# First stage of a transformer block: q, k and v from two fp32r parts in three products, the norm on ScalarE

## The chip, the cores and the metric

One core of a Trainium2 chip runs the whole program. The metric is the device time of one execution, in microseconds.

## The reference

```python
h = _layernorm(x, axis=-1) * (1 + ca) + sa
x = x + ga * _L0_attn_ref(h, w_qkv, w_proj, b_proj)
...
def _L0_attn_ref(x, w_qkv, w_proj, b_proj):
    qkv = (x @ w_qkv).reshape(B, S, 3, heads, head_dim)
    Q, K, V = (qkv[:, :, 0], qkv[:, :, 1], qkv[:, :, 2])
    Q = apply_rope(Q)
    K = apply_rope(K)
    ...
```

`x` is (4, 2048, 256) in f32, `w_qkv` (256, 768), and there are 16 heads of 16. Attention, the projection and a mixture of experts follow; they are the other stages of the kernel and are left as they are, but for the increments named below. The change bears on the layer norm, its modulation with `ca` and `sa`, and the product with `w_qkv`.

## The kernel before

The program is a row of stages: setup (`setup_stage`), q, k and v (`qkv_stage`), attention, middle (projection, second norm, routing), experts, shared expert. Each stage is a block of its own, which begins on all five engines when the one before has ended. Within a stage every engine has its own list of instructions, in an order written out by hand, and semaphores tie them together.

`qkv_stage` goes over 16 units of 512 tokens (4 batches, 4 units each), and a unit over 4 tiles of 128 tokens. `steps_of` (L308) calls `run` once a unit on each engine; batches 1 and 2 are a hardware loop. Within `run`, step t handles several tiles at once: `tile(t, k)` is the tile k steps back, of this unit or the one before. What a tile goes through:

- `products` (TensorE, L614), step n: h times `wqkv`, 2 chunks of 128 for q and k (512 columns, to `ps_qk`) and 2 for v (256 columns, to `ps_v`), in f32. It waits for the rotation of the tile two before and for `h_t` of its unit.
- `rope` (VectorE, L513), step n: the rotation, three operations out of `ps_qk` into `rot_c` and `rot_s`.
- `take_v` (ScalarE, L563), step n: v out of PSUM. `add` (GpSimd, L464), step n: the sum of the two halves of the rotation, `qk`.
- `turn_qk` (TensorE, L628), two steps later: four transposes of `qk` into `ps_x`, which has two slots. It waits for `rest` of the tile two before it.
- `first` (ScalarE, L570), two steps later, `leave` (VectorE, writes `rest`, L528), `second` (ScalarE, L577) and `third` (GpSimd, L470), three steps later: q and k split into three bf16 parts.

Once a unit, for the next unit: `stat` (VectorE, L493) takes mean and variance, `rstds` (GpSimd, L457) the reciprocal root, `normalise` (VectorE, L504) writes `xn`, `turn_h` (TensorE, L605) transposes it with eight transposes into `ps_ht`, and `modulate` (ScalarE, L555) writes `h_t`, two activations of 128x512. Before the change `stat` stands after the rotation of tile 0, `rstds` after the sum of tile 0, `normalise` after step 1 of VectorE, and `turn_h` at the end of step 2 of TensorE:

```python
def run(b, s, more, tile):      # VectorE, L535
    for t in range(TPS):
        if tile(t, 0):
            rope(b * SPB + s, t, s * TPS + t)
        if t == 0 and more:
            stat(b * SPB + s + 1, (s + 1) % SPB, b + ((s + 1) // SPB + 1))
        if tile(t, 3):
            u, tt, slot, _ = tile(t, 3)
            leave(u, tt, slot)
        if t == 1 and more:
            normalise(b * SPB + s + 1, (s + 1) % 2, (s + 1) % SPB)
```

`stand_alone` (L161) is an increment of a semaphore that nobody waits for.

## Time and profile before

| | us |
|---|---|
| median of 3 runs (lowest to highest) | 3309.3 (3305.76 to 3310.84) |
| the profiled execution, its own time | 3308.82 |
| its span, from first to last instruction | 3307.1 |
| PE busy (TensorE matmul) in the span | 2912.5 (88%) |
| DVE busy (VectorE) | 2518.0 (76%) |
| ACT busy (ScalarE) | 1588.5 (48%) |
| POOL busy (GpSimd) | 884.5 (27%) |
| mean granted TensorE clock, share of full speed | 0.944 |

The shares of the whole span mix six stages. The first stage runs from 29.4 us to near 300; the first 40 us of it and the last 20 are its ends. A busy PE is not PE at its peak, since matmuls are pipelined and their ends are modelled. Spans on POOL are rough. In rows, idle time and what ended it stand in brackets behind an instruction.

### The profile page before, as it was taken

How to read it: one execution, taken by the hardware profiler on the slowest of the kernel's cores; microseconds unless marked ns; L12 is line 12 of the kernel's file. 1: busy time of each engine (PE TensorE's matmuls, PEld its weight loads, DVE VectorE, ACT ScalarE, POOL GpSimd, SP SyncE). 2: the span in 40 equal slices, each digit the busy share in tenths (PEclk: the TensorE clock that was granted, in tenths of full speed). 3: DMA queues.
4: the chain of work that ended last, by engine and by line, in shares of the span. 5: the costliest groups of instructions: out<-in, count | busy, mean ns of one | idle time of the engine just before them, and what ended most of it. 6: DMA issues, size and time to landing. Idle time of an engine off the chain costs nothing. (4 is left out here: it accounts for less than half of the span.)

```text
span 3307.1 us, 61435 instructions
## 1 busy us (share of the span) xinstructions
PE 2912.5 (88%) x22508; PEld 1616.0 (49%) x22508; DVE 2518.0 (76%) x4678; ACT 1588.5 (48%) x2160; POOL 884.5 (27%) x1100
## 2 busy tenths in 40 slices
PE   6885699999999999999999996873999999788888
PEld 3553133333333333333333325763888888677776
DVE  5885989888898888898888914664777777566665
ACT  2542166666676666666666782221444444111111
POOL 5773010111110111101111112664222222333332
PEclk8997699999999999999999997775999999899999
DMA  4776111122111212111221005664444455332332
GB/s 132 204 209 186 49 35 47 48 54 53 43 44 49 54 48 57 38 46 48 55 52 43 20 8 160 212 198 167 155 155 155 156 159 156 105 94 85 96 97 73
DMA packets 388533, 317.93 MB, mean 96 GB/s; under 512 B 112720, under 2 KB 374844, under 8 KB 388288
## 3 DMA queue, kind: packets, MB, share of 16 engines
q1 hardware_dynamic: 370752, 277.67, 29.4%
q0 software_dynamic: 12288, 33.57, 3.0%
q10 hardware_dynamic: 5248, 3.41, 0.4%
q8 instruction: 155, 2.54, 0.3%
q14 instruction: 90, 0.74, 0.1%
HBM read 196.89 MB, written 116.93 MB: 95 GB/s over the span
## 5 line engine op out<-in xcount | busy, mean ns | idle before, releaser
L903 ACT ACTIVATE probs<-ps_s 128x1024 f32<-128x1024 f32 (+3 forms) x1280 | 1077.9, 896 | 599.2 <-PE ps_s L1071 598.6
L926 DVE TENSOR_REDUCE piece_rest<-ps_m 128x1 f32<-128x512 f32 (+2 forms) x1260 | 748.8, 646 | 91.8 <-PE ps_m L1046 42.0
L1071 PE MATMUL ps_s<-q_st,k_st 50*128 50x512 bf16 (+7 forms) x5120 | 594.4, 346 | 19.0 <-ACT probs L903 15.2
L1086 PE MATMUL ps_o<-probs,vs 128*32 128x512 f32 (+3 forms) x5120 | 600.8, 541 | 4.3 <-POOL probs L883 1.2
L883 POOL TENSOR_SCALAR_AFFINE_SELECT probs<-probs 128x256 f32<-128x256 f32 x512 | 204.9, 406 | 1481.2 <-ACT probs L903 1476.0
L926 DVE TENSOR_REDUCE piece_late<-ps_m 128x1 f32<-128x512 f32 x900 | 548.8, 666 | 33.0 <-PE ps_m L1038 17.9
L1038 PE MATMUL ps_m<-k_st,q_st 48*128 48x512 bf16 (+3 forms) x2400 | 407.5, 353 | 65.8 <-DVE piece_rest L926 48.1
L1038 PEld LDWEIGHTS ps_m<-k_st,q_st 48*128 48x128 bf16 x2400 | 106.9, 93 | 651.8 <-DVE piece_rest L926 339.0
L1071 PEld LDWEIGHTS ps_s<-q_st,k_st 50*128 50x128 bf16 (+1 forms) x5120 | 224.1, 95 | 250.8 <-ACT probs L903 91.0
L1803 ACT ACTIVATE act_g<-ps_g 128x512 f32<-128x512 f32 x117 | 69.9, 597 | 279.5 <-PE ps_u L1895 279.5
L1840 DVE TENSOR_TENSOR hid_f<-act_g,ps_u 128x512 f32<-128x512 f32 x117 | 80.5, 688 | 126.8 <-ACT act_g L1803 126.8
L1086 PEld LDWEIGHTS ps_o<-probs,vs 128*32 128x32 f32 x5120 | 101.2, 108 | 142.8 <-issue 96.9
L2086 ACT ACTIVATE act_g<-ps_g 128x512 f32<-128x512 f32 x80 | 47.5, 595 | 251.1 <-PE ps_u L2191 206.3
L1765 POOL TENSOR_TENSOR wu_low<-wu,wu_high 128x768 fp32r<-128x768 f32 x39 | 76.8, 1968 | 326.1 <-ACT wu_high L1791 326.1
L2202 PE MATMUL ps_d<-sd_high,hid_high 128*128 128x256 f32 x384 | 114.0, 297 | 47.5 <-DVE hid_low L2135 46.2
L1359 POOL DMA_INDIRECT expert_rows<-rows,at x128 | 133.3, 1041 | 66.9 <-issue 36.0
L1845 DVE TENSOR_TENSOR hid_low<-hid_f,hid_high 128x512 fp32r<-128x512 f32 x117 | 138.8, 1187 | 4.0
L2051 POOL DMA_INDIRECT got<-expert_made,at_now x128 | 128.7, 1006 | 49.1 <-issue 36.8
L1907 PE MATMUL ps_d<-wd_high,hid_high 128*128 128x256 f32 x468 | 136.0, 291 | 1.2 <-DVE hid_low L1845 1.2
L1907 PE MATMUL ps_d<-wd_low,hid_high 128*128 128x256 f32 x468 | 132.1, 282 | 0.0
L1907 PE MATMUL ps_d<-wd_high,hid_low 128*128 128x256 f32 x468 | 132.0, 282 | 0.0
L621 PE MATMUL ps_qk<-wqkv,h_t 128*128 128x512 f32 x256 | 122.8, 603 | 1.0 <-ACT h_t L559 1.0
(228 smaller groups left out, 5103.2 us busy)
## 6 DMA issues: line engine op xcount, KB each, us to landing
k_st<-qk_parts SPq DMA_DIRECT2D x768, 32.0 KB, 1.8
qk_parts<-parts SPq DMA_DIRECT2D x124, 192.0 KB, 2.9
q_st<-qk_parts SPq DMA_DIRECT2D x720, 32.0 KB, 1.8
x_r<-expert_rows SPq DMA_DIRECT2D x39, 512.0 KB, 4.6
expert_made<-made SPq DMA_DIRECT2D x39, 512.0 KB, 2.9
x_in<-in_L_attn_x_dram SPq DMA_DIRECT2D x32, 512.0 KB, 4.7
vs<-v_ones SPq DMA_DIRECT2D x64, 256.0 KB, 3.7
v_ones<-v_out SPq DMA_DIRECT2D x60, 256.0 KB, 4.7
```

The costliest lines, as they stand in the source:

```text
L621: pe.matmul(ps_qk[:, t % 2, :], h_t[:, slot, c, t * P:(t + 1) * P], wqkv[:, c, 0:QK], start=(c == 0), stop=(c == DC - 1))
L883: pool.affine_select(out=block_now, in_=block_now, compare_op=ALU.is_ge, fill=0.0, base=0, pattern=[[0, 2], [1, P]], channel_multiplier=-1 ...
L903: act.activation(probs[:, u % PSLOTS, 2 * pair:2 * pair + 2, j * P:ST], ps_s[:, pair, :, j * P:ST], ACT.Exp, scale=SCALE).then_inc(exp_don ...
L926: v.tensor_reduce(dst, ps_m[:, bank, 0:n * w].rearrange("p (n w) -> p n w", n=n), AX.X, ALU.max) \
L1038: last[z] = pe.matmul(bank[:, i * w:(i + 1) * w], q_st[rows, slot, 0, a + i, qi * P:(qi + 1) * P], k_st[rows, slot, 0, a + i, kt * ST:kt * ...
L1071: last = pe.matmul(ps_s[:, pair, z, j * P:ST], k_st[rows, slot, half, pair, kc * P:(kc + 1) * P], q_st[rows, slot, half, pair, qt * ST + j ...
L1086: last = pe.matmul(ps_o[h * VW:(h + 1) * VW, j * P:ST], vs[:, slot, kc, h * VW:(h + 1) * VW], probs[:, u % PSLOTS, h, j * P:ST], start=(kc ...
L1359: pool.indirect_dma_start(rows_dram, bass.IndirectOffsetOnAxis(at[:, rslot, j:j + 1], 0), rows[:, rslot, j % TPS, :], None).then_inc(scatt ...
L1845: v.tensor_tensor(hid[1][:, i, :], hid_f[:, half, :], hid[0][:, i, :], ALU.subtract).then_inc(hid_done, 1)
L1907: last = pe.matmul(ps_d[:, t, :], hid[a][:, i, t * P:(t + 1) * P], wd_p[b][:, slot, i, :], start=(i == 0 and t % 2 == 0 and k == 0), stop= ...
L2051: pool.indirect_dma_start(got[:, slot, j, :], None, made_dram, bass.IndirectOffsetOnAxis(at_now[:, slot, j:j + 1], 0)) \
L2202: last = pe.matmul(ps_d[:, slot, t, :], hid[a][:, i % GS, t * P:(t + 1) * P], wd_p[b][:, i, :], start=(i == 0 and t % 2 == 0 and k == 0), ...
```

## The change

`wqkv` and h are each split into two fp32r parts, "high" (rounded) and "low" (the remainder), and the product is taken as high x high + high x low + low x high: six matmuls where two f32 matmuls stood, for q and k and for v. For it `modulate` writes h twice (`h_p[0]` in fp32r and `h_f` in f32), now one chunk at a time, the first at the end of step 1 and the second in step 2, and `low_rows` on VectorE subtracts the two at the end of step 2, one 128x512 operation a chunk; `products` waits for it. The weights are split in the setup stage, on ScalarE and GpSimd.

The norm goes from VectorE to ScalarE, as `x * rstd + shift`, at the start of step 0. VectorE only makes `shift`, four elements a partition, at the start of step 0 before `rope`; `xn` has one slot. `stat` and `rstds` work two units ahead, in step 3: `stat` before the rotation of tile 3, `rstds` after the sum of tile 3, where it also waits for the norm before. `turn_h` goes from the end of step 2 to the end of step 1. In the middle and the shared stage all increments of `held` are taken out (six places).

```diff
-                    wqkv=first.enter_context(nc.sbuf_tensor("wqkv", [P, DC, 3 * D], F32)),
+                    wqkv=[first.enter_context(nc.sbuf_tensor(f"wqkv_{part}", [P, DC, 3 * D], F32R)) for part in PARTS],
+                    w_raw=first.enter_context(nc.sbuf_tensor("wqkv_raw", [P, DC, 3 * D], F32)),
...
+            pool.wait_ge(masks, 6)
+            pool.wait_ge(exp_done, 2)
+            pool.tensor_tensor(Q["wqkv"][1][:, :, :], Q["w_raw"][:, :, :], Q["wqkv"][0][:, :, :], ALU.subtract)
...
+            act.wait_ge(Q["consts"], 16 * 3)
+            act.activation(Q["wqkv"][0][:, :, :], Q["w_raw"][:, :, :], ACT.Copy).then_inc(exp_done, 1)
...
-        xn = sb("xn", [P, 2, TPS, D])
-        h_t = sb("h_t", [P, 2, DC, ST])
+        xn = sb("xn", [P, TPS, D])
+        h_p = [sb(f"h_{part}", [P, 2, DC, ST], F32R) for part in PARTS]
+        h_f = sb("h_f", [P, DC, ST])
+        shift = sb("shift1", [P, TPS])
...
                 pool.wait_ge(pool_own, u + 3)
+                if not (isinstance(u, int) and u == 0):
+                    pool.wait_ge(xn_done, u * TPS)
+                    stand_alone(pool, held)
                 pool.tensor_tensor(rstd[:, :], var[:, :], power[:, :], ALU.pow).then_inc(rstd_done, 1)
...
-                    if t == 0 and more:
-                        rstds(b * SPB + s + 1)
+                    if t == 3 and has(2):
+                        rstds(b * SPB + s + 2)
                     if tile(t, 3):
                         u, tt, slot, _ = tile(t, 3)
                         third(u, tt, slot)
...
-            def normalise(u, slot, x_slot):
+            def shifts(u):
                 v.wait_ge(rstd_done, u + 1)
-                for t in range(TPS):
-                    ins = v.tensor_scalar(xn[:, slot, t, :], x_in[:, x_slot, t, :], mv[:, t, 0:1], rstd[:, t:t + 1],
-                                          ALU.subtract, ALU.mult)
-                    ins.then_inc(xn_done, 1)
-                v.wait_ge(xn_done, (u + 1) * TPS)
-                v.sem_inc(x_read, 1)
+                v.scalar_tensor_tensor(shift[:, :], mv[:, :, 0], -1.0, rstd[:, :], ALU.mult, ALU.mult) \
+                    .then_inc(shift_done, 1)
+
+            def low_rows(u, slot, c):
+                v.wait_ge(ht_done, u * DC + (c + 1 + 2))
+                v.tensor_tensor(h_p[1][:, slot, c, :], h_f[:, c, :], h_p[0][:, slot, c, :], ALU.subtract).then_inc(h_low, 1)
...
+                    if t == 0 and has(1):
+                        shifts(b * SPB + s + 1)
+                    if t == 3 and has(2):
+                        stat(b * SPB + s + 2, (s + 2) % SPB, b + ((s + 2) // SPB + 1))
                     if tile(t, 0):
                         rope(b * SPB + s, t, s * TPS + t)
-                    if t == 0 and more:
-                        stat(b * SPB + s + 1, (s + 1) % SPB, b + ((s + 1) // SPB + 1))
                     if tile(t, 3):
                         u, tt, slot, _ = tile(t, 3)
                         leave(u, tt, slot)
-                    if t == 1 and more:
-                        normalise(b * SPB + s + 1, (s + 1) % 2, (s + 1) % SPB)
+                    if t == 2 and has(1):
+                        for c in range(DC):
+                            low_rows(b * SPB + s + 1, (s + 1) % 2, c)
...
+            def modulate(u, slot, b, c):
+                act.wait_ge(ht_turned, u * DC + (c + 1))
+                act.wait_ge(h_low, u * DC + (c + 1))
+                stand_alone(act, held)
+                act.activation(h_p[0][:, slot, c, :], ps_ht[:, c, :], ACT.Identity,
+                               bias=mod_t[:, M_SA + c, ds(b, 1)], scale=mod_t[:, M_CA + c, ds(b, 1)])
+                act.activation(h_f[:, c, :], ps_ht[:, c, :], ACT.Identity,
+                               bias=mod_t[:, M_SA + c, ds(b, 1)], scale=mod_t[:, M_CA + c, ds(b, 1)]) \
+                    .then_inc(ht_done, 1)
+
+            def normalise(u, slot, x_slot):
+                act.wait_ge(shift_done, u + 1)
+                stand_alone(act, held)
+                for t in range(TPS):
+                    act.activation(xn[:, t, :], x_in[:, x_slot, t, :], ACT.Identity,
+                                   bias=shift[:, t:t + 1], scale=rstd[:, t:t + 1]).then_inc(xn_done, 1)
+                act.wait_ge(xn_done, (u + 1) * TPS)
+                act.sem_inc(x_read, 1)
...
-                    if t == 2 and more:
-                        modulate(b * SPB + s + 1, (s + 1) % 2, b + (s + 1) // SPB)
+                    if t == 0 and has(1):
+                        normalise(b * SPB + s + 1, (s + 1) % 2, (s + 1) % SPB)
                     if tile(t, 0):
                         take_v(b * SPB + s, t, s % 2, b * 2 + (s // 2 + 1))
+                    if t == 2 and has(1):
+                        modulate(b * SPB + s + 1, (s + 1) % 2, b + (s + 1) // SPB, 1)
                     if tile(t, 2):
                         first(*tile(t, 2))
                     if tile(t, 3):
                         u, tt, slot, _ = tile(t, 3)
                         second(u, tt, slot)
+                    if t == 1 and has(1):
+                        modulate(b * SPB + s + 1, (s + 1) % 2, b + (s + 1) // SPB, 0)
...
                 if t == 0:
-                    pe.wait_ge(ht_done, u * DC + (DC + 2))
+                    pe.wait_ge(h_low, u * DC + 2 * DC)
                 pe.wait_ge(rope_done, n + TPS - 1)
                 pe.wait_ge(v_done, n + 1)
...
+                terms = [(c, a, b) for c in range(DC) for a, b in PRODUCTS]
+                for k, (c, a, b) in enumerate(terms):
+                    pe.matmul(ps_qk[:, t % 2, :], h_p[a][:, slot, c, t * P:(t + 1) * P], wqkv[b][:, c, 0:QK],
+                              start=(k == 0), stop=(k == len(terms) - 1))
...
-                    if t == 2 and more:
+                    if t == 1 and has(1):
                         turn_h(b * SPB + s + 1, (s + 1) % 2)
...
-                stand_alone(pool, held)
```

How the instructions of VectorE stand in a row, between `rest` of one step and the next: before, from step 0 of a unit on (`rot_c` and `rot_s` are the rotation, STATS and AGGR the statistics, `xn` the norm).

```order
L521 TENSOR_TENSOR rot_c<-ps_qk,cos 128x512
L522 TENSOR_TENSOR rot_s<-ps_qk,sin 128x32x8
L524 TENSOR_TENSOR rot_s<-ps_qk,sin 128x32x8
L496 BN_STATS stats<-x_in 128x6 x4
L501 BN_AGGR mv<-stats 128x2 x4
L532 TENSOR_TENSOR rest<-ps_x,parts 128x512
L521 TENSOR_TENSOR rot_c<-ps_qk,cos 128x512
L522 TENSOR_TENSOR rot_s<-ps_qk,sin 128x32x8
L524 TENSOR_TENSOR rot_s<-ps_qk,sin 128x32x8
L532 TENSOR_TENSOR rest<-ps_x,parts 128x512
L507 TENSOR_SCALAR xn<-x_in,mv,rstd 128x256 x4
```

Of the change, VectorE from the end of step 2 to the end of the next unit's step 0 (lines are the changed kernel's; `h_low` is the subtraction of `low_rows`):

```order
L525 TENSOR_TENSOR h_low<-h_f,h_high 128x512 x2
L510 BN_STATS stats<-x_in 128x6 x4
L515 BN_AGGR mv<-stats 128x2 x4
L535 TENSOR_TENSOR rot_c<-ps_qk,cos 128x512
L536 TENSOR_TENSOR rot_s<-ps_qk,sin 128x32x8
L538 TENSOR_TENSOR rot_s<-ps_qk,sin 128x32x8
L546 TENSOR_TENSOR rest<-ps_x,parts 128x512
L520 SCALAR_TENSOR_TENSOR shift<-mv,rstd 128x4
L535 TENSOR_TENSOR rot_c<-ps_qk,cos 128x512
L536 TENSOR_TENSOR rot_s<-ps_qk,sin 128x32x8
L538 TENSOR_TENSOR rot_s<-ps_qk,sin 128x32x8
L546 TENSOR_TENSOR rest<-ps_x,parts 128x512
```

The statistics stood behind the rotation of tile 0 and now stand ahead of that of tile 3; `shift` stands ahead of the rotation of tile 0.

GpSimd before, from the `third` in step 3 of one unit to the sum in step 1 of the next (`qk` is the sum, `parts` is written by `third`, `var` and `rstd` by `rstds`):

```order
L472 TENSOR_TENSOR parts<-rest,parts 128x4x128
L468 TENSOR_TENSOR qk<-rot_c,rot_s 128x512
L460 TENSOR_SCALAR var<-mv 128x4
L462 TENSOR_TENSOR rstd<-var,power 128x4
L472 TENSOR_TENSOR parts<-rest,parts 128x4x128
L468 TENSOR_TENSOR qk<-rot_c,rot_s 128x512
```

Of the change, GpSimd from the `third` in step 2 to the sum in step 0 of the next unit:

```order
L485 TENSOR_TENSOR parts<-rest,parts 128x4x128
L481 TENSOR_TENSOR qk<-rot_c,rot_s 128x512
L470 TENSOR_SCALAR var<-mv 128x4
L475 TENSOR_TENSOR rstd<-var,power 128x4
L485 TENSOR_TENSOR parts<-rest,parts 128x4x128
L481 TENSOR_TENSOR qk<-rot_c,rot_s 128x512
```

The pieces read alike, but the sum ahead of `var` was that of tile 0 and is now that of tile 3.

## Rows read from the trace of the kernel before

**Rows 1.** VectorE timeline (start us, us, what, count, idle before): tiles 2, 2, 3.

```profile
52.23 0.69 DVE L521 TENSOR_TENSOR rot_c<-ps_qk,cos 128x512 f32<-128x512 f32 x1 [0.66 <-DVE xn L507]
...
265.28 0.69 DVE L521 TENSOR_TENSOR rot_c<-ps_qk,cos 128x512 f32<-128x512 f32 x1 [0.23 <-DVE xn L507]
...
280.57 0.69 DVE L521 TENSOR_TENSOR rot_c<-ps_qk,cos 128x512 f32<-128x512 f32 x1 [1.07 <-PE ps_v L624]
```

**Rows 2.** Windows: us, busy PE, PEld, DVE, ACT, POOL, clock, DMA share, GB/s.

```profile
67.04:265.28 198.24, 176.53 (x730) 109.78 (x730) 162.89 (x364) 95.29 (x182) 142.10 (x130) 1.00 0.75 204
```

**Rows 3.** TensorE's timeline, two ordinary tiles and a late one.

```profile
101.00 1.88 PE L621 MATMUL ps_qk<-wqkv,h_t 128*128 128x512 f32 x4
...
103.58 0.60 PE L633 MATMUL ps_x<-ident,qk 128*128 128x128 f32 x4
104.02 1.88 PE L621 MATMUL ps_qk<-wqkv,h_t 128*128 128x512 f32 x4
...
107.65 0.66 PE L633 MATMUL ps_x<-ident,qk 128*128 128x128 f32 x4 [0.88 <-DVE rest L532]
```

**Rows 4.** VectorE's timeline, a tile with the statistics.

```profile
103.78 0.69 DVE L521 TENSOR_TENSOR rot_c<-ps_qk,cos 128x512 f32<-128x512 f32 x1 [1.07 <-PE ps_v L624]
...
105.05 1.39 DVE L496 BATCH_NORM_STATS2 stats<-x_in 128x6 f32<-128x256 f32 x4
...
106.90 0.69 DVE L532 TENSOR_TENSOR rest<-ps_x,parts 128x512 f32<-128x512 f32 x1
107.51 0.68 DVE L521 TENSOR_TENSOR rot_c<-ps_qk,cos 128x512 f32<-128x512 f32 x1
```

**Rows 5.** TensorE's timeline in the shared stage, first and last of each width.

```profile
2900.14 0.28 PE L2202 MATMUL ps_d<-sd_high,hid_low 128*128 128x256 f32 x1
...
2901.20 0.28 PE L2202 MATMUL ps_d<-sd_high,hid_low 128*128 128x256 f32 x1
...
2902.48 0.39 PE L2191 MATMUL ps_g<-h_high,sg_low 128*128 128x512 f32 x1
```

**Rows 6.** GpSimd's timeline, sum, var, root and third part.

```profile
105.31 1.27 POOL L468 TENSOR_TENSOR qk<-rot_c,rot_s 128x512 f32<-128x512 f32 x1 [0.70 <-DVE rot_s L524]
107.18 0.23 POOL L460 TENSOR_SCALAR var<-mv 128x4 f32<-128x4 f32 x1 [0.60 <-DVE mv L501]
107.49 1.04 POOL L462 TENSOR_TENSOR rstd<-var,power 128x4 f32<-128x4 f32 x1
108.50 1.16 POOL L472 TENSOR_TENSOR parts<-rest,parts 128x512 bf16<-128x512 f32 x1
```

**Rows 7.** Timelines of VectorE and GpSimd, norm alone and beside sum.

```profile
35.23 1.38 DVE L507 TENSOR_SCALAR xn<-x_in,mv,rstd 128x256 f32<-128x256 f32 x4 [3.44 <-POOL rstd L462]
...
109.36 3.21 DVE L507 TENSOR_SCALAR xn<-x_in,mv,rstd 128x256 f32<-128x256 f32 x4
...
109.62 1.32 POOL L468 TENSOR_TENSOR qk<-rot_c,rot_s 128x512 f32<-128x512 f32 x1
...
L507 DVE TENSOR_SCALAR xn<-x_in,mv,rstd x1: 1358/1358/1358, 109.7 to 109.7; 128x256 f32<-128x256 f32 x1
```

**Rows 8.** Source view: middle stage's shift; count, ns min/median/max, first and last.

```profile
L1437 DVE SCALAR_TENSOR_TENSOR shift<-mv,rstd x16: 161/164/164, 2026.3 to 2239.7; 128x4 f32<-128x4 f32 x16
```

**Rows 9.** Timelines in the expert stage, GpSimd's subtraction and VectorE's.

```profile
2706.03 1.97 POOL L1769 TENSOR_TENSOR wd_low<-wd,wd_high 128x768 fp32r<-128x768 f32 x1 [1.39 <-ACT wd_high L1794]
...
2706.33 2.21 DVE L1845 TENSOR_TENSOR hid_low<-hid_f,hid_high 128x512 fp32r<-128x512 f32 x1
```

**Rows 10.** ScalarE: the middle stage's norm, and h in the first.

```profile
L1398 ACT ACTIVATE xn<-x,shift,rstd x64: 583/592/601, 2026.5 to 2241.8; 128x256 f32<-128x256 f32 x64
...
113.21 1.45 ACT L559 ACTIVATE h_t<-ps_ht,mod_t 128x512 f32<-128x512 f32 x2 [3.11 <-PE ps_ht L611]
```

**Rows 11.** GpSimd's timeline, start of the first stage.

```profile
29.46 3.52 POOL L449 MEMSET v_out<- 128x4096 f32 x1 [13.64 <-POOLq L169]
```

**Rows 12.** Windows view, 50 us of the middle stage.

```profile
2150.00:2200.00 50.00, 42.36 (x242) 35.58 (x242) 32.85 (x169) 15.87 (x34) 32.97 (x34) 0.72 0.74 217
```

46 lines of the change are left out of this document (16 added, 30 removed).

## Prediction

> **What bounds the stage now.** Only the first stage changes, so I read that stretch alone, one cycle of 512 tokens at a time. A unit's cycle can be timed by the first rotation of its tile 2: from 52.23 us (unit 0) to 265.28 (unit 14) are 14 cycles, 15.22 us each [rows 1]. Inside these cycles the windows view gives PE 176.5 busy of 198.2 us, DVE 162.9, POOL 142.1, ACT 95.3 [rows 2]: PE leads, but is not full. The PE rows show both halves of that [rows 3]. An ordinary tile takes 3.02 us (101.00 to 104.02), of which 2.58 are the four products in two passes each and 0.44 the four transposes; four tiles and eight transposes of h (0.88) make 13.0. The other 2.2 us of a cycle are waits for VectorE, such as the 0.88 us for `rest` before 107.65. VectorE is late there because it does the statistics (105.05 to 106.90) ahead of `rest` [rows 4], and later the norm: four operations take 3.21 us beside GpSimd, against 1.38 when GpSimd is idle [rows 7].
>
> **The change, part by part.** The profiled execution took 3308.8 us (0.5 below the median of the runs shown), and the sum is made against it.
>
> *Products.* The shared stage's fp32r products issue every 0.118 us for 256 columns (nine steps from 2900.14 to 2901.20) and every 0.232 us for 512 (then one step of 0.12 and five of 0.232 up to 2902.48) [rows 5]. Six of each are 2.10 us a tile in place of 2.58. PE's own work falls to 4 x (2.10 + 0.44) + 0.88 = 11.0 us a unit. By itself that would be worth 2 us a unit.
>
> *VectorE.* It loses the norm (3.2) and gets one small `shift` (0.16 [rows 8]) and two `low_rows` subtractions of 128x512. Such an operation takes 0.69 us with nothing in its way (`rot_c` of the same width, [rows 4]). A tile's rotation takes 1.27 us and its `rest` 0.61 before the next begins [rows 4]. So 4 x 1.88 + 1.85 + 0.15 + 1.38 = 10.9 us of work.
>
> *GpSimd* keeps 4 x (1.27 + 1.16) and the reciprocal root at 1.38: 11.1 us. *ScalarE* gets four norms of 0.59 and two more activations of h, at 0.72 each [rows 10]; its 7.3 of today (95.3 in 13 cycles [rows 2]) less the two of h is 5.9, so it comes to 11.2. No engine's work, then, is over 11.2 us where a cycle is 15.2.
>
> *The order.* What decides is what waits for what, and here the rows of the order in the change's section matter. The statistics of unit u+2 now stand before the rotation of tile 3, the root behind GpSimd's sum of tile 3, and `shift` before the rotation of the next tile 0. VectorE can't begin that rotation until GpSimd has done the sum and the root, both of which need the rotation of tile 3. And PE's transposes of h now stand one tile earlier, behind the transposes of tile 3 of the unit before; these need `rest` of tile 1, which VectorE does after the rotation of tile 0. So one ring runs through every cycle, with nothing to break it. From the start of PE's products of tile 2, in us:
>
> - products 2.10, and 0.20 until the rotation starts (103.58 to 103.78): 2.30
> - rotation of tile 2 and one `rest`: 1.88, so 4.18
> - two `low_rows`: 1.38, so 5.56
> - statistics (105.05 to 106.90): 1.85, so 7.41
> - rotation of tile 3 until GpSimd's sum starts (103.78 to 105.31 [rows 4, 6]): 1.50, so 8.91
> - sum of tile 3: 1.27, so 10.18
> - var and root, 107.18 to 108.53 and 0.03 ahead [rows 6]: 1.38, so 11.56
> - `shift`: 0.15, so 11.71
> - rotation of tile 0 (1.27) and `rest` of tile 1 to its end (0.69): 13.67
> - transposes start 0.06 later (107.59 to 107.65 [rows 3, 4]); four of tile 3 and eight of h, 1.32: 15.05.
>
> This is a floor under the cycle: 15.05 against 15.22. The matmuls save 0.48 us of it, once, and nothing of what they save in the other three tiles counts.
>
> *What meets on GpSimd.* Before the change the second norm of a unit was issued at 109.7, right behind the start of GpSimd's sum (109.62 to 110.94), and took 1.36 us, to the sum's end [rows 7]; in the expert stage `hid_low`, a subtraction of that width with both inputs in SBUF, is issued 0.3 us into one of GpSimd's and ends 0.54 after it: 2.21 us [rows 9]. The first `low_rows` is issued at 4.18 and GpSimd's sum of tile 2 runs from about 3.8 (it may be 0.3 later, the queue behind it being full) to 5.3. It then ends near 5.9, not 4.87: +1.0. The second meets `third` only if the second part of `rest` is ready by then. ScalarE has two activations of h for each half ahead of it there, so I expect it later and take 0; the bound above is one `third`, 1.16. `shift` is the open one. In [rows 6] `third` starts at 108.50, 0.03 before the root ends, while a waiting VectorE operation needs 0.04 after it (35.19 to 35.23, [rows 7]). `third` would thus be first, every time. A row of `shift` beside a busy GpSimd doesn't exist; bounds are 0 (0.16 in all, [rows 8]) and one `third` less the 0.04 and a start, 1.1. I take 1.1, as both kinds of VectorE operation that the rows show there are held to the end of GpSimd's.
>
> The Trainium skill, "SBUF — State Buffer", section "Who interferes with whom", says that a VectorE instruction with two SBUF inputs and a GpSimd instruction that reads SBUF exclude each other for a whole instruction, and that the earlier one wins. By it `shift`, with `mv` and `rstd` in SBUF, is held for all of `third`: a cycle of 17.1. If only large operations were held, it would be 16.0. The rows of `hid_low` and of the norm agree with the rule; none shows it for four elements.
>
> So a cycle is 15.05 + 1.0 + 1.1 = 17.1 us.
>
> *The ends.* The first unit has four norms on ScalarE (2.1 for 1.4), two more activations of h (1.4) and two `low_rows` (1.4) before its first product, +3 us; its products are shorter even at half clock, and the transposes of unit 1 come a tile earlier, -3: 0, give or take 2. Unit 15 has no statistics and no ring: rotation of tile 2 in unit 14 to rotation of tile 3 in unit 15 was 15.29 [rows 1], and is 4.3 (with `low_rows`) + 2.3 + 3 x 2.54 = 14.2: -1. The setup gets an activation of 128x1536 on ScalarE and a subtraction on GpSimd (twice the 1.97 of [rows 9]); GpSimd was idle for 13.6 us before 29.46 [rows 11], so both are free; without that cover 4 us. The increments of a semaphore that other stages lose (some 100 in all) lie beside waits; I count 0 and at most 3 us.
>
> **Sum.** 14 x (17.1 - 15.22) = 26.3; with the ends -1, and 3308.8: 3334, which I round up to 3335 for the waits on registers that the loop adds.
>
> **The rivals.**
> 1. *`shift` isn't held*: cycle 16.0, 14 x 0.78 - 1 = +10: 3319. For it: it has four elements a partition. Against: the two operations of the rows that are held.
> 2. *The second `low_rows` is held too*: 18.2, +41: 3350. It decides if ScalarE delivers the second part within 0.1 us of the first `low_rows`' end.
> 3. *The clock falls.* PE has 11.0 us of work in 17.1, with a gap of near 3 us before the transposes of tile 3. If that takes its granted clock from 2.4 to 1.2 GHz, the products (2.10) and transposes (1.32) of the ring double: +3.4 a cycle, 3382 if in every one, 3358 if in half of them. For it: in the middle stage PE is busy 42.4 of 50 us, more than here, and its granted clock averages 0.72 [rows 12]. Against: the first stage stands at 1.00 [rows 2], and its products are broad. The Trainium skill, "TensorE: Matmul & The Clock Gate", section "HAM oscillation — how this bites in real kernels", says that waits between bursts of matmuls can drop the clock in each pass of a loop, so that each burst starts at half speed; the middle stage's row agrees.
> 4. *No hold at all*: the floor, 14 x -0.17 - 1 = -3: 3305. It needs GpSimd idle where [rows 6] has it busy.
> 5. *Faster: the ring is open, and the stage goes at its busiest engine.* If the root of unit u+2 were there when VectorE comes to `shift`, and `rest` of tile 1 when PE comes to tile 3, the cycle would be the 11.2 us of work: 14 x -4.0 - 1 = -57: 3252. For it: all engines have that little to do, and every product comes 0.48 us earlier. It decides at `shift`: the sum and the root (2.65 us) would have to fit beside one `rest` (0.61). I see no way in the queues, but a slip in my reading of the order would land here.
>
> **Chances.** Forecast (17.1) 0.37; rival 1 0.16; rival 2 0.12; rival 3 0.16; rival 4 0.08; rival 5 0.11. A measurement of this kernel tells changes of about 0.2% (6.6 us) from none. Slower by more are the forecast and rivals 1 to 3: 0.81; within it rival 4: 0.08; faster 0.11. The range leaves out rival 5 and the worse half of rival 3 and takes in the rest with the uncertainty of the ends: 3303 to 3360.
>
> **What would show it.** In the changed kernel: rotations of tile 2 some 17 us apart; a VectorE wait of about 2 us for the root at `shift`, and a `shift` of 1.2 instead of 0.16 us; the first `low_rows` of a unit at 1.5 us or more and the second at 0.69; a PE wait for `rest` before the transposes of tile 3, some 2 us; products at 0.232 and 0.118 us apart with the clock at 1.00. A cycle under 15 us would prove the ring wrong, and with it the forecast; a cycle of 16 with a `shift` of 0.16 is rival 1.

## The result, and the profile after

The changed kernel takes 3370.7 us (median of 4 runs, 3362.9 to 3380.4) against 3310.1 in the runs beside it: ratio 1.0185, 95% interval 1.0155 to 1.0214. It is slower, as forecast, but by 61 us and not 25, and it lies above the range of 3303 to 3360. Its profiled execution took 3370.5 us with a span of 3368.8 (before: 3308.8 and 3307.1), at a mean granted clock of 0.934 (before 0.944).

First the busy times of the changed kernel, from the head of its page:

```profile
span 3368.8 us, 62012 instructions
...
PE 2911.0 (86%) x22764; PEld 1668.3 (50%) x22764; DVE 2527.3 (75%) x4662; ACT 1637.0 (49%) x2257; POOL 895.5 (27%) x1101
```

TensorE is busy for as long as before (2911.0 against 2912.5), though its work in the first stage became smaller. Nothing is to be had from this line. What helps is to cut both spans at the same landmarks. The views of three tiles give for each matmul line its count, ns (min/median/max), first and last start in us. Before the change (attention's output, the experts' and the shared stage's first product):

```profile
L1086 PE MATMUL ps_o<-probs,vs x5120: 272/592/1061, 395.1 to 1987.0; 128*32 128x512 f32 x137, 128*32 128x384 f32 x20, 128*32 128x256 f32 x20, 128*32 128x128 f32 x20
...
L1895 PE MATMUL ps_g<-x_t_high,wg_high x234: 389/396/763, 2296.7 to 2823.9; 128*128 128x512 f32 x117
...
L2191 PE MATMUL ps_g<-h_high,sg_high x192: 393/395/764, 2853.1 to 3293.6; 128*128 128x512 f32 x192
```

and after it:

```profile
L1119 PE MATMUL ps_o<-probs,vs x5120: 272/592/1045, 430.7 to 2022.4; 128*32 128x512 f32 x137, 128*32 128x384 f32 x20, 128*32 128x256 f32 x20, 128*32 128x128 f32 x20
...
L1923 PE MATMUL ps_g<-x_t_high,wg_high x234: 395/396/767, 2348.7 to 2876.4; 128*128 128x512 f32 x117
...
L2216 PE MATMUL ps_g<-h_high,sg_high x192: 389/395/765, 2906.4 to 3355.3; 128*128 128x512 f32 x192
```

The differences of these numbers are a table of stages:

| stretch | before | after | difference |
|---|---|---|---|
| to attention's first output (first stage) | 395.1 | 430.7 | +35.6 |
| attention | 1591.9 | 1591.7 | -0.2 |
| middle stage, to the first expert product | 309.7 | 326.3 | +16.6 |
| experts | 556.4 | 557.7 | +1.3 |
| shared stage | 440.5 | 448.9 | +8.4 |
| end | 13.5 | 13.5 | 0 |

So there are two things to explain. The first stage lost 35.6 us where I had 25, and two stages in which the change takes out only some increments of a semaphore lost 25 more.

**The first stage.** The ring of the prediction is there, link by link. One passage from GpSimd's root to the transposes, timelines of all engines after the change (start, duration, what, idle before it):

```profile
165.63 1.04 POOL L475 TENSOR_TENSOR rstd<-var,power 128x4 f32<-128x4 f32 x1 [0.26 <-POOL var L470]
...
166.64 1.16 POOL L485 TENSOR_TENSOR parts<-rest,parts 128x512 bf16<-128x512 f32 x1
...
166.70 1.12 DVE L520 SCALAR_TENSOR_TENSOR shift<-mv,rstd 128x4 f32<-128x4 f32 x1 [2.37 <-POOL rstd L475]
...
167.74 0.68 DVE L535 TENSOR_TENSOR rot_c<-ps_qk,cos 128x512 f32<-128x512 f32 x1
167.94 2.07 ACT L586 ACTIVATE xn<-x_in,shift,rstd 128x256 f32<-128x256 f32 x4 [2.94 <-DVE shift L520]
...
169.00 0.68 DVE L546 TENSOR_TENSOR rest<-ps_x,parts 128x512 f32<-128x512 f32 x1
...
169.83 0.41 PE L666 MATMUL ps_x<-ident,qk 128*128 128x128 f32 x2 [2.61 <-DVE rest L546]
```

VectorE stands 2.37 us for the root, `third` (L485) starts 0.06 us ahead of `shift`, and `shift` takes 1.12 us for four elements a partition, where the middle stage's takes 0.16 [rows 8]. TensorE's next instructions, the transposes of `qk` and of h, start only behind `rest`, after 2.61 us idle. The views of the two lines that could be held beside GpSimd, over the whole stage:

```profile
L520 DVE SCALAR_TENSOR_TENSOR shift<-mv,rstd x16: 164/1114/1123, 35.5 to 290.6; 128x4 f32<-128x4 f32 x16
...
L525 DVE TENSOR_TENSOR h_low<-h_f,h_high x32: 677/1669/1840, 40.0 to 302.1; 128x512 fp32r<-128x512 f32 x32
```

`shift` and the first `low_rows` of a cycle are held in all cycles but the first; both holds are as large as forecast. The windows view of four whole cycles (the columns are those of [rows 2]) then shows what was not in the sum:

```profile
149.66:166.70 17.04, 12.07 (x76) 10.36 (x75) 12.68 (x27) 10.10 (x20) 11.42 (x11) 1.00 0.60 164
217.70:235.70 18.00, 13.05 (x74) 11.08 (x73) 13.64 (x27) 10.10 (x20) 10.82 (x11) 0.91 0.74 197
235.70:253.70 18.00, 11.75 (x75) 10.08 (x74) 13.63 (x28) 10.10 (x20) 10.90 (x11) 1.00 0.64 175
253.70:272.80 19.10, 14.30 (x72) 12.14 (x71) 13.29 (x28) 10.29 (x20) 11.20 (x11) 0.82 0.62 164
```

The first is 17.04 us long, against 17.1 predicted. The third is a whole microsecond longer with the clock at 1.00 all the same. What differs is the second `low_rows` and GpSimd's `third` beside it. In the first cycle and then in the third:

```profile
158.29 2.35 DVE L525 TENSOR_TENSOR h_low<-h_f,h_high 128x512 fp32r<-128x512 f32 x2
159.95 1.72 POOL L485 TENSOR_TENSOR parts<-rest,parts 128x512 bf16<-128x512 f32 x1 [0.45 <-ACT parts L607]
...
244.35 3.27 DVE L525 TENSOR_TENSOR h_low<-h_f,h_high 128x512 fp32r<-128x512 f32 x2
245.92 1.15 POOL L485 TENSOR_TENSOR parts<-rest,parts 128x512 bf16<-128x512 f32 x1 [0.45 <-ACT parts L607]
```

Both times the two start within 0.03 us of each other (the second `low_rows` at 159.97 and 245.95). At 159.95 `third` is the one held (1.72 us) and the second `low_rows` takes 0.68; at 245.92 `third` takes its 1.15 and the second `low_rows` is held, 1.67. That is rival 2 of the prediction, in some of the cycles.

From the `shift` at 45.6 us (the second; the one before it belongs to the start) to the last at 290.6 there are 14 cycles, 17.5 us on the average. One is 15.2 (the first), six are 16.8 to 17.0, five 17.8 to 18.1 and two 19.1 and 19.3. In the seven from 17.8 up both `low_rows` are held, in the others only one. The clock leaves its upper level in six of these seven and in none of the others. Where it falls once (four cycles of 17.8 to 18.1) a cycle is no longer than the third one above, which has no fall; where it falls twice (the two of 19.1 and 19.3, mean 0.82) it costs 1.1 and 1.3 us more. So most of the surplus is the hold, and the clock adds the rest in two cycles.

### The profile page after: what moved, and what is told of

Read it like the earlier page. It is cut to its first block and busy times, and to the rows that moved or that the text cites. A ratio compares the mean times of both kernels' runs of the same rounds, so it can differ in the third digit from the quotient of the medians.

```text
span 3368.8 us, 62012 instructions
## 1 busy us (share of the span) xinstructions
PE 2911.0 (86%) x22764; PEld 1668.3 (50%) x22764; DVE 2527.3 (75%) x4662; ACT 1637.0 (49%) x2257; POOL 895.5 (27%) x1101
## 5 line engine op out<-in xcount | busy, mean ns | idle before, releaser
L1104 PE MATMUL ps_s<-q_st,k_st 50*128 50x512 bf16 (+7 forms) x5120 | 594.4, 346 | 19.0 <-ACT probs L936 15.2
L959 DVE TENSOR_REDUCE piece_late<-ps_m 128x1 f32<-128x512 f32 x900 | 549.2, 667 | 32.7 <-PE ps_m L1071 17.1
L1079 PE MATMUL ps_m<-mask,ident 64*128 64x128 bf16 x1920 | 113.1, 215 | 0.0
```

What stands on the lines that cost most here:

```text
L959: v.tensor_reduce(dst, ps_m[:, bank, 0:n * w].rearrange("p (n w) -> p n w", n=n), AX.X, ALU.max) \
L1104: last = pe.matmul(ps_s[:, pair, z, j * P:ST], k_st[rows, slot, half, pair, kc * P:(kc + 1) * P], q_st[rows, slot, half, pair, qt * ST + j ...
```

## The experiments

Fifteen kernels ran, in four groups. The kernel before was run beside each group (3311.0 to 3313.5 us). The state of knowledge at the start: my theory for the first stage was the ring with its two holds and a clock that falls in part of the cycles (the third hold, shown above, was not in it); for the other stages, that the increments are worth what those stages lost. The rival for both is drift: the clock or the moment at which a stage begins.

### The increments, alone and put back

`held` is a semaphore on which nobody waits. An increment of it stands between a wait and the instruction that needs it. b_mid takes the four of the middle stage out of the kernel before, b_shared the two of the shared stage:

```diff
 middle stage, GpSimd
-                stand_alone(pool, held)
                 for j in range(TOPK * TPS):
                     pool.indirect_dma_start(rows_dram, ...
...
                     pool.wait_ge(stat_done, u + 2)
-                    stand_alone(pool, held)
...
 middle stage, VectorE, ahead of bn_aggr and of max_index
-                stand_alone(v, held)
```

> The kernel before with one edit: the four increments of `held` in the middle stage are gone (first and second stage, experts and shared stage as before). Theory (increments): in the change, the middle stage lost 16.6 us (attention's end to the first expert product: 310.8 us before, 327.4 after), because each removed increment lets its wait travel with the operation behind it. Then this kernel is slower than before by the same: 3310 + 16.6 = 3326.7 us, with the units of the middle stage 15.5 to 16 us apart, as after the change, in place of 14.5. Rival (drift): the middle stage of the change lost its time to the TensorE clock or to where it began; then this kernel takes 3310 us within 3 us. My forecast in the prediction was 0 to 3 us for all removed increments together.

Measured: 3329.1 us, ratio 1.0057 (1.0043 to 1.0070), 17.4 over the median beside it.

> The kernel before with one edit: the two increments of `held` in GpSimd's gather of the shared stage are gone. Theory (increments): the 8.4 us that the shared stage lost in the change are theirs: 3310 + 8.4 = 3318.5 us, units of the shared stage 28.1 us apart in place of 27.5. Rival (drift): 3310 us within 3 us, and the 8.4 us were the TensorE clock, 0.95 after against 0.98 before in that stage.

Measured: 3322.3 us, ratio 1.0032 (1.0019 to 1.0045), 10.6 over it. From the first to the last ps_g are 449.8 us in its profile (2854.1 to 3303.9), 440.5 before and 448.9 after the change.

a_held does the reverse: the changed kernel with all six put back.

> The changed kernel with the removed increments put back in the middle and the shared stage (one semaphore for the whole program stands for the three of before, since three are too many beside the two new ones of the first stage). Theory (increments): all that stage one did not cost comes back: 3370.7 - 16.6 - 8.4 = 3345.7 us, that is 35.5 us over the kernel before, all of it in the first stage. Rival (drift): no change, 3370 us within 4.

Measured: 3342.8 us, ratio 1.0092 (1.0076 to 1.0108). 27.9 of the 61 us come back. Its middle stage takes 311.4 us (309.7 before, 326.3 after the change) and its shared stage 436.7. Drift is out for the greater part. All profiles of this document with the increment ahead of the writes have a middle stage of 308.8 to 317.7 us, all without it one of 324.1 to 334.3; and in the medians the increments cost 17 and 11 us on a kernel whose first stage nobody touched, and they give 28 back on the other. What is left over the kernel before, 31 us, is the first stage.

### Which increment, and why it matters

m_gather removes only the increment ahead of the eight indirect writes in the middle stage; m_vector removes only VectorE's two.

> The kernel before without one increment: the one ahead of GpSimd's eight indirect writes of expert_rows in the middle stage (all four removed cost 17.4 us of 3311.7). Theory (scatter): the writes of a unit start later behind their own wait, and they and the root share GpSimd's queue, so that the next unit's norm comes late; this one increment carries most of it: 3311 + 14 to 17 = 3325 to 3328 us. Rival (VectorE's): 3311 within 3.

Measured: 3329.2 us, ratio 1.0057 (1.0043 to 1.0070).

> The kernel before without the two increments on VectorE in the middle stage (ahead of the second statistics and of max_index). In the run without all four, each unit's wait there is shorter by 0.11 us, not longer (2.4 to 0.6 and 2.5 to 0.6 us in 16 units). Theory (scatter on GpSimd carries the loss): 3311 us or up to 3 less. Rival (VectorE's carry it, by where its instructions then start beside GpSimd's): 3320 and up.

Measured: 3314.9 us, ratio 1.0008 (0.9999 to 1.0017). (Its one profiled execution has a middle stage of 315.4 us, 5.7 longer than before, of which the medians show 1.4; that is inside the spread just given.)

One increment of four carries the loss. But it is no simple delay. The groups of GpSimd's writes in the middle stage, before and then in m_gather (busy us, mean ns, idle before):

```profile
L1359 POOL DMA_INDIRECT expert_rows<-rows,at x128 | 133.3, 1041 | 66.9 <-issue 36.0 <-DVE at L1473 30.9
```
```profile
L1358 POOL DMA_INDIRECT expert_rows<-rows,at x128 | 128.9, 1007 | 78.9 <-DVE at L1472 44.4 <-issue 34.3 <-DMA expert_rows<-rows,at 0.3
```

The wait for `at` is longer without the increment, yet the first write of a unit follows `at` sooner: 0.46 us after its start, against 1.02 with the increment, in nearly every unit. GpSimd itself gains half a microsecond. The loss is TensorE's. Its wait for ScalarE's evacuation of h ahead of ps_l, before and then in m_gather (groups from 2025 us to the stage's end):

```profile
L1616 PE MATMUL ps_l<-gate_t,h 128*128 128x8 f32 x247 | 33.8, 272 | 12.9 <-ACT h L1404 9.5 <-issue 3.4
```
```profile
L1615 PE MATMUL ps_l<-gate_t,h 128*128 128x8 f32 x243 | 41.7, 308 | 26.6 <-ACT h L1403 20.6 <-issue 6.0
```

It doubles, from 12.9 to 26.6 us in all, and the products of ps_l get slower besides (272 to 308 ns in the mean), since the clock is lower behind the wait: a product takes 0.26 us at a granted clock of 1.00 and 0.36 at 0.50, and m_gather has six units near 0.50 where the kernel before has none (the last two units, slow in both, left out). These two, 13.7 and 7.9 us, are about the 21.8 us by which the middle stage of this profile is longer. Why ScalarE is late shows in the timelines of one unit. Before:

```profile
2116.43 1.04 PE L1611 MATMUL ps_h<-ident,rows 128*128 128x128 f32 x8
2116.56 0.96 POOL L1359 DMA_INDIRECT expert_rows<-rows,at  x1 [0.30 <-issue]
...
2117.13 0.60 ACT L1404 ACTIVATE h<-ps_h 128x512 f32<-128x512 f32 x1 [6.37 <-issue]
...
2117.82 0.96 POOL L1359 DMA_INDIRECT expert_rows<-rows,at  x1 [0.30 <-issue]
2117.93 0.60 ACT L1404 ACTIVATE h<-ps_h 128x512 f32<-128x512 f32 x1 [0.21 <-PE ps_h L1611]
```

and in m_gather:

```profile
2122.62 1.04 PE L1610 MATMUL ps_h<-ident,rows 128*128 128x128 f32 x8
...
2123.30 0.96 POOL L1358 DMA_INDIRECT expert_rows<-rows,at  x1 [0.30 <-issue]
...
2124.46 0.60 ACT L1403 ACTIVATE h<-ps_h 128x512 f32<-128x512 f32 x1 [7.01 <-PE ps_h L1610]
...
2125.87 0.60 ACT L1403 ACTIVATE h<-ps_h 128x512 f32<-128x512 f32 x1 [0.82 <-remote]
...
2126.52 3.49 PEld L1615 LDWEIGHTS ps_l<-gate_t,h 128*128 128x128 f32 x16 [3.10 <-ACT h L1403]
2126.52 3.58 PE L1615 MATMUL ps_l<-gate_t,h 128*128 128x8 f32 x16 [2.86 <-ACT h L1403]
```

Before, the first evacuation starts 0.7 us after the transposes begin, in all units at full clock. In m_gather it starts 1.8 to 2.0 us after them in four units, each time 0.05 to 0.2 us behind the end of GpSimd's last write (here 2124.26), and in eight units the second starts 2.0 us or more after them instead of by 1.2 to 1.5. In the kernel before, the last write of a unit ends 1.9 us or more after the transposes' start, when both evacuations are under way. That is a coincidence seen in all four cases. The first evacuation also waits for a store of h from two units back (the one for this slot was issued at 2095.92, 27 us before); the second waits for the transposes alone, which end at 2123.66 here, and it too is late. For that wait the profile knows no instruction of this core that ends it ("remote"). What holds ScalarE there I can't name.

The next two kernels ask what it is about the increment. m_ahead moves it in front of the waits; m_two puts two in its place.

```diff
 m_ahead
+                stand_alone(pool, held)
                 pool.wait_ge(at_done, u + 2)
                 if not (isinstance(u, int) and u < 2):
                     pool.wait_ge(scattered[(rslot + 2) % RSLOTS], turn * SCATTER)
-                stand_alone(pool, held)
                 for j in range(TOPK * TPS):
```

> The kernel before; the increment ahead of GpSimd's eight indirect writes in the middle stage is moved, not removed: it stands ahead of the two waits in place of behind them, so that GpSimd has as many instructions and the last wait stands directly ahead of the writes again. Without it the first write began 0.46 us after `at` was begun, with it 1.02, and yet the stage took 16 us more. Theory (what parts wait and write matters): as without it, 3311 + 16 = 3327 us, and 0.46 us from `at` to the first write. Rival (the place or number of GpSimd's instructions matters): 3311 within 4.

Measured: 3328.1 us, ratio 1.0044 (1.0029 to 1.0060). The first write starts 0.46 us after `at` again, and TensorE waits 21.7 us ahead of ps_l. Here the first evacuation is late in one unit only (1.05 us behind the transposes' start), the second in eight (1.8 to 3.2 us). In b_mid the first is late in two (1.76 and 1.86) and the second in six. So what the three kernels share is the late second evacuation; the four cases of m_gather are not needed for the loss.

> The kernel before with two increments in place of one between the waits and the eight indirect writes. Theory (part wait and write): the second changes nothing but its own issue, 3311 within 3, and 1.0 to 1.1 us from `at` to the first write. Rival (the later start itself is the gain): the writes begin later again by what an increment takes, and the stage gains or loses more than 4 us by it.

Measured: 3313.6 us, ratio 1.0004 (0.9995 to 1.0012). The first write starts 1.11 us after `at`; TensorE waits 12.8 us ahead of ps_l.

The number of GpSimd's instructions and their place in the code are excluded by m_ahead: the same increment is worth 15 us behind the waits and nothing ahead of them. A second one changes nothing. Whether the parting as such matters, or the 0.56 us by which the writes then come later, these kernels don't tell apart, since whatever parts the two also delays the writes.

> The kernel before without one of the two increments in the gather of the shared stage, that between the wait for at_now's copy and the eight indirect gathers (both removed cost 10.6 us). Theory (the same as in the middle stage, an increment between a wait and an indirect DMA): it carries the loss, 3311 + 8 to 11 = 3320 to 3322 us. Rival (the one ahead of the copy carries it): 3311 within 3.

Measured: 3322.8 us, ratio 1.0037 (1.0024 to 1.0050), 9.4 over the median beside it. In the shared stage too it is the increment directly ahead of indirect DMAs. With it (kernel before) and without it (b_shared), GpSimd's timeline:

```profile
3000.68 0.39 POOL L2046 COPY at_now<-made_at 128x8 uint32<-128x8 uint32 x1
3001.88 0.99 POOL L2051 DMA_INDIRECT got<-expert_made,at_now  x1 [0.81 <-POOL at_now L2046]
```
```profile
3003.93 0.39 POOL L2044 COPY at_now<-made_at 128x8 uint32<-128x8 uint32 x1
3004.59 1.27 POOL L2048 DMA_INDIRECT got<-expert_made,at_now  x1 [0.27 <-POOL at_now L2044]
```

The picture is the same: without the increment the first gather starts 0.54 us sooner behind the copy, and the stage is 9 us longer. Through which wait I did not follow there. That the middle stage's loss goes through ScalarE's evacuation is read from its traces; why a sooner write makes that late stays open in both stages.

### Opening the ring

The prediction says that the root comes too late for `shift`. a_early moves statistics and root one step up, on the changed kernel:

```diff
 GpSimd
-                    if t == 3 and has(2):
+                    if t == 2 and has(2):
                         rstds(b * SPB + s + 2)
 VectorE
-                    if t == 3 and has(2):
+                    if t == 2 and has(2):
                         stat(b * SPB + s + 2, (s + 2) % SPB, b + ((s + 2) // SPB + 1))
```

> The changed kernel with the statistics on VectorE and sum and root on GpSimd one step earlier (step 2 in place of 3), all else as in the change. Theory (ring): VectorE idles 2.37 us ahead of every `shift` for GpSimd's root (18.8 us in 8 units), because statistics, rotation of tile 3, its sum, the root and `shift` follow one upon the other. A step earlier the root is done long before `shift`, and a cycle loses 2.35 us of its 17.5: 15.1, over 14 cycles -33 us, 3338 us, with VectorE (13.1 us busy of a unit) next in line. Rival (engine-bound): VectorE takes the work in the same order of need, the 2.35 us reappear as waits for ps_v or ps_x (PE waits 44 us for `rest` already): 17.0 a cycle, 3365 to 3371 us. Half of it: 16.3, 3354.

Measured: 3383.1 us, ratio 1.0204 (1.0188 to 1.0221): 12 us over the change's median, though the two intervals overlap; what is sure is that it isn't faster. All three expectations missed. This kernel also lacks the increments, as the change does. The wait at `shift` did go, but the groups of VectorE from 150 to 290 us show what took its place:

```profile
L510 DVE BATCH_NORM_STATS2 stats<-x_in 128x6 f32<-128x256 f32 x28 | 9.8, 413 | 31.0 <-DMA x_in<-in_L_attn_x_dram 31.0
...
L520 DVE SCALAR_TENSOR_TENSOR shift<-mv,rstd 128x4 f32<-128x4 f32 x7 | 1.9, 266 | 0.0
```

31.0 us of waits for the load of x_in, in seven units. The load needs 4.4 us to land, but SyncE issues it behind the eight stores of q and k (6.4 us of issuing from 147.12, then the load at 153.76; 4.4 us later, at 158.16, the statistics begin). In the change the same load was 6 us early (issued at 149.9, statistics at 160.6), and so it stood in no view as a wait. It was the next ring, one behind the other: the stores wait for `third`, the load is queued behind the stores, and the statistics wait for the load. TensorE's clock then fell to 0.83 in that stretch.

h_open therefore opens both: statistics and root earlier (the root behind `third` now), and each load one unit earlier, which the four slots of x_in allow since the unit they held is normalised by then. It stands on the version with the increments put back, as do all kernels below whose names begin with h.

```diff
 setup, SyncE
-            for u in range(SPB - 1):
+            for u in range(SPB):
                 sp.dma_start(Q["x_in"][:, u, :, :], ...
 first stage, SyncE
-                    if not (last_batch and s >= 1):
-                        load(u + 3, (s + 3) % SPB)
+                    if not last_batch:
+                        load(u + SPB, s)
```

> The changed kernel with its increments restored (3342.8 us), and the ring opened at both places: statistics and root one step earlier (step 2, the root behind `third`), and x_in loaded one unit earlier (all four slots in the setup, then unit u+4 where u+3 was), since in the run with the earlier statistics alone VectorE stood 31 us in 7 units for the DMA of x_in. Theory (ring): the cycle falls from 17.5 to what the engines have to do, VectorE's 13.1 us of a unit and its waits for ps_v 1.8: 14.8, 14 cycles -38, 3305 us. Rival (the ring only hides the next wait): PE waits for `rest` and h_low as before, 17 a cycle, 3335 to 3343. Rival (clock): the cycle falls to about 16, since the granted clock stays under 1.00 with TensorE at 11 us of work: 3322.

Measured: 3286.3 us, ratio 0.9922 (0.9905 to 0.9939). It beats its own base by 56 us and the kernel before by 25. The windows view of 100 us of it, and VectorE's groups from 60 to 225 us:

```profile
100.00:200.00 100.00, 84.17 (x539) 74.34 (x538) 95.25 (x202) 74.92 (x150) 83.33 (x74) 1.00 0.87 232
```
```profile
L526 DVE TENSOR_TENSOR h_low<-h_f,h_high 128x512 fp32r<-128x512 f32 x24 | 36.1, 1544 | 0.0
...
L536 DVE TENSOR_TENSOR rot_c<-ps_qk,cos 128x512 f32<-128x512 f32 x49 | 33.2, 677 | 5.9 <-PE ps_v L658 5.9
...
L521 DVE SCALAR_TENSOR_TENSOR shift<-mv,rstd 128x4 f32<-128x4 f32 x12 | 11.1, 922 | 0.0
```

After the first, a cycle is 13.5 to 13.8 us, VectorE is 95% busy, and the clock stays at 1.00. Both `low_rows` are held in every one of these cycles, and `shift` is too. All three expectations missed; the kernel is faster than each. The 14.8 of the first had counted waits for ps_v (1.8 us a unit) as fixed; they shrank to 0.5 with the rest. The earlier load alone was not tried, nor the earlier statistics with the root ahead of `third` and the load early.

h_pshift leaves the order as the change has it and computes `shift` on GpSimd, right behind the root:

```diff
 GpSimd, in rstds
+                pool.tensor_scalar(minus[:, :], mv[:, :, 0], -1.0, None, ALU.mult)
                 pool.tensor_scalar(var[:, :], mv[:, :, 1], EPS, None, ALU.add).then_inc(pool_own, 1)
...
                 pool.tensor_tensor(rstd[:, :], var[:, :], power[:, :], ALU.pow).then_inc(rstd_done, 1)
+                pool.wait_ge(rstd_done, u + 1)
+                pool.tensor_tensor(shift[:, :], minus[:, :], rstd[:, :], ALU.mult).then_inc(shift_done, 1)
 VectorE
-                    if t == 0 and has(1):
-                        shifts(b * SPB + s + 1)
```

> The changed kernel with its increments restored (3342.8 us), `shift` taken from VectorE to GpSimd: minus the mean beside the variance, and one product right behind the root. Theory (hold): `shift` costs 1.12 us on VectorE because it starts 0.06 us behind GpSimd's `third`; on GpSimd it costs some 0.3 us ahead of `third`, and 0.8 us of a cycle go: -11, 3332 us. Rival (the hold moves): the rotation of tile 0, next on VectorE, is held by `third` in its place: 3343 within 3.

Measured: 3321.2 us, ratio 1.0030 (1.0018 to 1.0043): 22 us less than its base where I expected 11. Its timeline shows that more than a hold went:

```profile
159.63 0.20 POOL L480 TENSOR_TENSOR shift<-minus,rstd 128x4 f32<-128x4 f32 x1
159.71 0.69 DVE L535 TENSOR_TENSOR rot_c<-ps_qk,cos 128x512 f32<-128x512 f32 x1 [1.06 <-PE ps_v L655]
159.78 1.16 POOL L490 TENSOR_TENSOR parts<-rest,parts 128x512 bf16<-128x512 f32 x1
159.95 2.08 ACT L584 ACTIVATE xn<-x_in,shift,rstd 128x256 f32<-128x256 f32 x4 [2.49 <-POOL shift L480]
```

VectorE's queue no longer has the wait for the root in it. The rotation of tile 0 starts when its products are there, and it isn't held by `third`, which runs beside it. The cycle is 16.3 us, and the clock stays at 1.00 throughout (61.8 to 273.9 us), where a_held's averaged 0.89. That is the part of the gain I hadn't counted. a_held's 14 cycles are 17.95 us in the mean: four of 15.0 to 17.0 with one `low_rows` held, and ten of 17.8 to 19.3 with both held and all the falls of the clock. In h_pshift only the second is held in each cycle after the first (0.78 and 1.57 us). How the 22 us divide between the two holds and the clock, this pair of kernels doesn't tell. The Trainium skill, "SBUF — State Buffer", section "Who interferes with whom", says that a VectorE instruction with at most one SBUF input, outside the two-port modes, doesn't contend with GpSimd; `rot_c`, with one input in PSUM, agrees (0.69 us beside `third`), and `shift`, with both in SBUF, agrees the other way (1.12 for 0.16).

### The parts of the change apart

h_order takes the three products out again and keeps the norm on ScalarE and the new order; b_products puts the three products alone into the kernel before, with `low_rows` in step 3.

> The changed kernel with its increments restored and the three fp32r products undone: fp32 products, one h_t and one evacuation of it, no `low_rows`, no parts of wqkv; the norm on ScalarE and the new order of steps stay. Theory (ring): the cycle is the ring without its two `low_rows` (1.4 + 1.4 held), 17.0 - 2.8 = 14.2, with TensorE's 13.0 us close under it; against 15.2 before, 14 cycles -14: 3297 us. Rival (TensorE): the ring's waits for fp32 products (3.3 in place of 2.7 of a tile) put it back to 15.2: 3311. Rival (the norm on ScalarE or the order is the loss): 16 or more, 3322 and up.

Measured: 3321.1 us, ratio 1.0028 (1.0015 to 1.0041). A cycle is 15.1 to 16.9 us, 16.0 in the mean of 13 (59.0 to 266.4), with the clock at 0.95. That is the third expectation by its number: in the closed ring the norm on ScalarE and the new order cost 10 us together, and the three products another 22. But the cycles say what the 10 us are. Seven of the 13 have the clock at 1.00 and take 15.1 to 15.2 us, no more than the old order's 15.22; in the other six it falls once, and they take 16.8 to 16.9. Six times 1.7 us are the 10. What makes the clock fall more in this order than in the old one was not looked into. The ring itself gives the 15.2: 17.04, less 2.35 for the pair of `low_rows`, and 0.48 for fp32's longer products of tile 2. My 14.2 subtracted both `low_rows` as held, 2.8 us, and left out the 0.48.

> The kernel before with the three fp32r products alone: two parts of h and wqkv, two evacuations a chunk on ScalarE, `low_rows` on VectorE in step 3; the norm stays on VectorE and the statistics where they were (increments as before, on one semaphore). Theory (VectorE): VectorE's 12.5 us of a unit become 15.3, and it is the bound: 16 to 17 us a cycle in place of 15.2, +11 to +25 us, 3322 to 3336. Rival (TensorE was the bound): TensorE's 13.0 us become 11.0, 14 a cycle, 3295. This shows what the norm on ScalarE and the order are worth beside the products: the change with increments took 3342.8.

Measured: 3396.1 us, ratio 1.0257 (1.0239 to 1.0274), 21 us a cycle. Even my theory's value was far too low. The chain of one unit explains it, from the waits view, 69.8 to 343.6 us (us in total, times, longest):

```profile
DVE rot_c L535 <- PE ps_v L645: 63.1, 26, 4.3
PE ps_qk L642 <- DVE h_low L525: 62.6, 13, 5.1
```

In step 3 `low_rows` stands directly ahead of the next unit's first products: TensorE waits 4.8 us for it a unit, and VectorE then up to 4.3 for the products. So this kernel tells what the three products cost in the old order with that placing, and not what they cost at best there. What it shows is why the change moved the transposes up: the products in parts need an evacuation, a subtraction and a wait more between the transposes and the first product.

h_order_open is the opened ring with fp32 products, h_open_p the opened ring with `shift` on GpSimd.

> The opened ring with fp32 products: the order of steps, the norm on ScalarE, the earlier statistics and loads stay; the three fp32r products, the second evacuation and `low_rows` are gone. VectorE's work is then 10.6 us of a unit and TensorE's 13.0. Theory (the products paid for themselves only where the ring is open): TensorE bounds, 14 us a cycle or more against 13.58, 15 cycles +6 or more: 3292 to 3300 us. Rival (the three products never pay): 13.0 to 13.3 a cycle, 3277 to 3284.

Measured: 3282.0 us, ratio 0.9906 (0.9891 to 0.9922).

> The opened ring (3286.3 us) with `shift` on GpSimd as well. In the opened ring a cycle takes 13.58 us and VectorE is busy 95 of 100 us: it is the bound now, and `shift` is 0.92 us of it, held. Theory (VectorE bound): the cycle falls by that, to 12.7, 15 cycles -13: 3273 us. Rival (GpSimd is next): it is busy 83 of 100 us and gets 0.5 us more in a unit, and PE waits for h_low 26.9 us in 12 units: -5 at the most, 3281 and up.

Measured: 3282.6 us, ratio 0.9914 (0.9899 to 0.9930).

h_order_open lies inside its rival's range: once the ring is open, the fp32 products are at least as good as the three fp32r products (3282.0 and 3286.3, with intervals that overlap). What TensorE saves, VectorE pays with `low_rows`. The first stage by itself is faster with fp32: its cycle is 12.95 us, nearly always, with TensorE busy for all of 100 us, against 13.58. Its profile comes to attention's first output 9.1 us sooner (360.2 against 369.3), of which 4.2 go again in the middle stage (317.7 against 313.5, both in the spread given above). So the three products pay in neither of these two orders.

h_open_p also lands in its rival's range. Its cycles take 13.6 us like h_open's, though VectorE is busy only 89 of 100 us there: waits for ps_v come in place of `shift` (18.0 us in 27 waits, against 5.9 in 13). So h_open's 13.6 is not VectorE's work alone; TensorE waits over 2 us a unit for `low_rows` in both. All three beat both kernels.

## Why the prediction was wrong

By its own steps:

- *The increments: "I count 0 and at most 3 us."* **This is the step that failed.** b_mid, b_shared and a_held measure 17.4, 10.6 and 27.9 us. I had put them beside waits, where an increment's own time is hidden. I asked only what they cost and not what they might be good for. The question for a removed instruction is also what it stood between: here a wait and an indirect DMA. No row of the kernel before shows what happens without it, so the bound should not have been one-sided.
- *The cycle: 15.05 + 1.0 + 1.1 = 17.1.* Six of 14 cycles take 16.8 to 17.04 us. In the one of 17.04 the wait for the root is 2.37 us, `shift` 1.12, the first `low_rows` 1.75 and the second 0.68; TensorE's wait for `rest` behind it is 2.61. Each was named in the list of what would show it, and h_open confirms the ring by breaking it. h_order confirms it without the `low_rows`: 15.1 to 15.2 us at full clock where the ring's sum gives 15.2.
- *The second `low_rows`: "I expect it later and take 0."* This term was wrong in half of the cycles. ScalarE's part is there by the first `low_rows`' end in every cycle of the forecast's kind, and `third` and the second `low_rows` start together; in seven of 14 cycles the second is held, for 1.0 us. That is rival 2 (18.2 a cycle; 17.97 measured with the clock at 1.00). I had made it an alternative for all cycles, while it is a near tie that falls either way.
- *The clock, rival 3.* It came true in two cycles, at +1.1 and +1.3 us. In four more it falls once and they are no longer than the held cycle without a fall. I had it as an alternative at +3.4, in all cycles or half of them. Holds and clock, less the first cycle, which was short (15.2), are the 14 x (17.5 - 17.1) = 5.6 us by which the cycles exceed the forecast. The rest of the first stage's surplus of 10.6 lies at its two ends, 35.6 - 14 x (17.5 - 15.22) = 3.7, which I had at -1. What makes them longer was not looked into.
- *"Setup free", attention and experts unchanged*: -0.2 and +1.3 us.
- *Rival 5*: it needs the root to be ready and gets none of it in this change, as said. But the price I gave it, 11.2 us a cycle, was too good: with the ring open it is 13.58, since VectorE's holds (0.9 a `low_rows` in the mean, 0.8 a `shift`) stay, and h_open_p shows that taking one of them away makes the cycle no shorter. h_order_open comes down to 12.95, TensorE's own work with fp32 products.

By terms, then: 25 forecast for the first stage and 35.6 measured, 0 forecast for the increments and 25 (in this profile) to 28 (in the medians) measured. The sum misses by 36 us, and the increments are 25 to 28 of them: with them put back the kernel takes 3342.8 us, 8 over the forecast.

## What to carry over

An operation that looks like an idle extra in a queue, such as an increment nobody waits for, may part a wait from the DMA behind it; take it out alone and time it before counting it at nothing. When a wait is removed, ask which queue feeds the next instruction: here the load, 6 us early and in no view of waits, became a wait of 4.4 us a unit as soon as the statistics moved. And a closed ring of small links across five queues hides all savings of work: shortening matmuls gave nothing, moving two instructions by a step and a load by a unit gave 56 us. Before a long cycle is put down to the clock, look for a long cycle without a fall: here it showed that the hold of one subtraction was the greater part.
